# A two-layer transformer kernel: exponentials in pairs, normalisations on ScalarE, a new placing of the small parts, and the first layer's rope rows by repeating transfers

## The reference

```python
# layer 0 attention, 16 heads of 8 dimensions, causal
c_kv = x @ W_kv_down
k_rope = rotary(c_kv @ W_k_rope)          # 32 dimensions, one for all heads
q_rope = rotary(x @ W_q_rope)
scores = q . k + q_rope . k_rope          # per head 8 + 32 dimensions
w = softmax(where(causal, -inf, scores / sqrt(40)))
out = (w @ v) @ W_o
# layer 0 ffn: a shared expert of 512 and 15 routed ones of 256, the best 3 by
# softmax weight, computed densely; plus the residual
# layer 1 attention: 16 heads of 8, no rope, not causal, grouped projections
# layer 1 ffn: 8 experts of 512, layer norm, each token goes to the best one
```

## Time and profile before

| | us |
|---|---|
| median of 3 runs | 984.2 (981.91 to 987.36) |
| profiled execution | 984.84 |
| its span, first to last instruction | 983.1 |
| lead | 0 to 61.1 |
| first layer's attention | 61.1 to 319.2 |
| dense experts | 319.2 to 558 |
| second layer's lead and attention | 558 to 841 |
| drain, blocks, end | 841 to 983.1 |
| PE, DVE, ACT, POOL busy | 792.4, 649.1, 524.2, 344.6 |

### The profile page before, as it was taken

How to read it: one execution, slowest core, us unless ns; L and a number is a source line. 1 busy time by engine, 2 the same in 40 slices (tenths; PEclk the granted TensorE clock), 3 DMA queues, 4 the chain that set the end, 5 groups by cost and what they waited for, 6 DMA issues and landing times. The chain is left out here.

```text
span 983.1 us, 12967 instructions
## 1 busy us (share of the span) xinstructions
PE 792.4 (81%) x4212; PEld 497.0 (51%) x4212; DVE 649.1 (66%) x1290; ACT 524.2 (53%) x970; POOL 344.6 (35%) x389
## 2 busy tenths in 40 slices
PE   3547888988898889999989899789989888527850
PEld 2233444555454667787767544345344444227740
DVE  3135568676663777776768696488898876347853
ACT  1013454545556677776757456456656656217740
POOL 3413775543532000000005345653453542133425
PEclk9987999999999999999999979899999999659985
DMA  4251331102110490000002112210110200011013
GB/s 125 48 95 21 85 81 35 34 22 46 30 24 2 137 285 6 1 1 1 1 8 57 43 42 63 60 35 17 38 25 18 58 4 10 4 54 56 32 34 84
DMA packets 56414, 44.75 MB, mean 46 GB/s; under 512 B 6598, under 2 KB 47387, under 8 KB 56347
## 3 DMA queue, kind: packets, MB, share of 16 engines
q1 hardware_dynamic: 55323, 41.82, 16.8%
q0 software_dynamic: 1024, 2.10, 0.7%
HBM read 14.67 MB, written 14.55 MB: 30 GB/s over the span
## 5 line engine op out<-in xcount | busy, mean ns | idle before, releaser
L926 ACT ACTIVATE ring<-single 128x512 f32<-128x512 f32 (+3 forms) x512 | 253.1, 517 | 226.3 <-PE single L1176 218.8
L1554 DVE TENSOR_REDUCE mneg<-pair 128x2 f32<-128x1024 f32 (+3 forms) x256 | 258.5, 1022 | 87.7 <-PE pair L1160 33.2
L1176 PE MATMUL single<-q_op,k_op 104*128 104x512 f32 (+3 forms) x512 | 216.5, 443 | 17.8 <-ACT ring L926 9.2
L1156 PE MATMUL pair<-k_op,q_op 96*128 96x512 f32 (+3 forms) x512 | 172.1, 415 | 42.2 <-DVE mneg L1554 22.6
L786 POOL TENSOR_SCALAR k_op<-k_stk,cst 104x512 fp32r<-104x512 f32 x64 | 100.0, 1577 | 276.2 <-DMA k_stk<-hl 258.5
L1176 PEld LDWEIGHTS single<-q_op,k_op 122*128 122x128 f32 (+1 forms) x512 | 97.9, 197 | 98.6 <-ACT ring L926 72.6
L1156 PEld LDWEIGHTS pair<-k_op,q_op 120*128 120x128 f32 (+1 forms) x512 | 98.9, 207 | 86.8 <-DVE mneg L1554 44.8
L1192 PE MATMUL p_o<-ring,vaug 128*9 128x512 f32 (+3 forms) x1024 | 116.1, 526 | 1.0 <-ACT ring L926 0.9
L721 POOL TENSOR_SCALAR_AFFINE_SELECT ring<-ring 128x256 f32<-128x256 f32 x128 | 52.3, 408 | 149.4 <-ACT ring L926 149.2
L955 ACT ACTIVATE ring<-pair,cols 128x512 f32<-128x512 f32 x136 | 86.1, 685 | 33.8 <-PE pair L1236 27.5
L1600 DVE TENSOR_TENSOR ring<-ring,single 128x1024 f32<-128x1024 f32 x60 | 73.3, 1221 | 45.5 <-ACT ring L955 44.4
(11 more groups left out here) (294 smaller groups left out, 1306.4 us busy)
## 6 DMA issues: line engine op xcount, KB each, us to landing
xs<-zero SPq DMA_DIRECT2D x10, 1024.0 KB, 10.1
q_op<-hl SPq DMA_DIRECT2D x96, 64.0 KB, 2.0
stage<-in_L_ffn_W_dram SPq DMA_DIRECT2D x8, 512.0 KB, 4.5
stage<-in_L_ffn_rW_dram SPq DMA_DIRECT2D x6, 512.0 KB, 5.1
k_op<-hl SPq DMA_DIRECT2D x48, 64.0 KB
k_stk<-hl SPq DMA_DIRECT2D x48, 64.0 KB, 2.0
xb<-xs SPq DMA_DIRECT2D x15, 128.0 KB, 2.0
xs<-yb SPq DMA_DIRECT2D x15, 128.0 KB, 1.7
```

Of the source, the lines that this page charges most:

```text
L926: exp_done.by(act.activation(ring[:, n % 8, lo:T], singles[n % 2][:, lo:T], ACT.Exp), (L, n))
L1156: ins = pe.matmul(both[:, i, 0:hi], r32(qs[:, P * qt:P * (qt + 1)]), r32(ks[:, 0:hi]), start=i == 0 or L == 1 or qt >= 2, stop=L == 1)
L1176: st_full.by(pe.matmul(singles[n % 2][:, lo:T], r32(ks[:, P * kc:P * (kc + 1)]), r32(qs[:, lo:T]), start=True, stop=True), (L, n))
L1554: s_taken.by(dve.tensor_reduce(mneg[:, G % 2, 2 * p:2 * p + 2, qt], both[:, :, 0:hi], axis=AX.X, op=ALU.max, negate=True), (L, m))
```

## The change

In the first layer:

- `exp_unit` and `exp` work on two heads at a time, in the `pair` buffers, two instructions a quad instead of four; `values` moves to the end of the quad's matmuls.
- `max_unit` uses the `single` buffers. A unit is two heads for the first two blocks of queries and one head for the last two: 12 units a group instead of 8. They stand two to five quads ahead.
- `rope_copy` and `qk_rope` are gone. `head_dma` sends the rope rows itself, by 6 transfers whose source is repeated four times (256 KB each), ahead of the group's 6 head transfers.
- The statistics and Newton steps of rows 1 to 3 are done together at the start of each layer (`BATCH`).

In both layers the application of a normalisation (`P.ne`, `T.ne`, `he`) moves from VectorE (L1392) to ScalarE, as four activations of 128 x 128 with bias and scale; VectorE computes the bias. `TABLE` is new. In the second layer the weight transfers and splits, all in row 0 before, are spread over the rows, at the rows' end on SyncE.

```diff
+SCORES = [[(heads, qt) for p in (0, 2) for heads, qt in (((p, p + 1), 0), ((p, p + 1), 1), ((p,), 2), ((p + 1,), 2), ((p,), 3), ((p + 1,), 3))],
+          [((p, p + 1), qt) for p in (0, 2) for qt in range(NT)]]
...
-        spread = (((-5, (0, 1, 2)), (-4, (3, 4, 5)), (-3, (6, 7))), ((-6, (0, 1)), (-5, (2, 3)), (-4, (4, 5)), (-3, (6, 7))))[L]
+        spread = (((-5, range(0, 4)), (-4, range(4, 7)), (-3, range(7, 10)), (-2, range(10, 12))),
+                  ((-6, (0, 1)), (-5, (2, 3)), (-4, (4, 5)), (-3, (6, 7))))[L]
...
-          (2, "b"): ["mt1", "P.ne"], (2, "d"): ["T.proj"], (3, "b"): ["P.ln1", "T.ns"], (3, "d"): ["P.rp", "T.na"],
...
+TABLE = [{(1, "b"): ["T.ot3"], (2, "b"): ["T.on"], (2, "d"): ["mt1", "U.rt2"], (3, "b"): ["T.proj", "P.ne"], (4, "b"): ["U.gt", "T.ns"],
...
+BATCH = {(0, "b"): "B.s1", (0, "d"): "B.s2", (1, "b"): "B.s3", (1, "d"): "B.sd", (2, "b"): "B.n1", (2, "d"): "B.n2", (3, "b"): "B.n3"}
...
             def head_dma(G):
...
+                if g < 3:
+                    taken.wait_ge(sp, ("rs", r))
+                    for w in range(2):
+                        for t in range(3):
+                            sp.dma_start((q_op0, k_op0)[w][DR * t:DR * (t + 1), GH * s:GH * s + GH, :],
+                                         rope_hl[DR * w:DR * (w + 1), TERM[w][t]:TERM[w][t] + 1, :].broadcast_to([DR, GH, T])).then_inc(rope_rows[s], 16)
...
-                ins = pool.tensor_copy(r32((q_op0, k_op0)[w][0:96, at:at + 2, :]), qk_rope[:, w:w + 1, :].broadcast_to([96, 2, T]))
...
+                    for t in range(NT):
+                        shift, scale = norm_of("P", s, t)
+                        ins = act.activation(xn[:, t, :], x[:, r, t, :], ACT.Identity, bias=shift, scale=scale)
...
-                exp_done.by(act.activation(ring[:, n % 8, lo:T], singles[n % 2][:, lo:T], ACT.Exp), (L, n))
+                    at = 2 * (n % 4)
+                    ins = act.activation(ring[:, at:at + 2, lo:T], pairs[n % 2][:, :, lo:T], ACT.Exp)
...
+                    if L == 0:
+                        exp_unit(L, Q, 0)
+                        for m in waiting[0:2]:
+                            max_unit(L, m)
+                        exp_unit(L, Q, 1)
+                        for name, b in beside_quad(s, q, "b"):
+                            part(name, b)
+                        for m in waiting[2:]:
+                            max_unit(L, m)
+                        if Q:
+                            values(L, Q - 1)
```

More of the change, by code:

```diff
@@ L176, in beside_quad @@
 def beside_quad(a, q, place):
[L177 to L180, removed]
+    L, lo = a // NB, a // NB * NB
+    out = [("wo0", 0)] if (a, q, place) == (0, 1, "d") else []
+    if a == lo and (q, place) in BATCH:
+        out.append((BATCH[q, place], L))
+    return out + [part for entry in TABLE[L].get((q, place), []) for part in named(entry, a, (lo, lo + NB))]
 def beside_unit(v):
     return [part for entry in BESIDE.get(v, [])
-            for part in named(entry, NB if entry[:2] == "T." else NB - 1, (NB - 1, NB + 1))]
+            for part in named(entry, NB if entry[:2] in ("T.", "U.") else NB - 1, (NB - 2, NB + 1))]
 def lead_parts(L):
@@ L403, in build @@
         k_masked = sig("k_masked", list(range(4 * NG)))
-        rope_rows = sem("rope_rows")
+        rope_rows = [sem(f"rope_rows{s}") for s in range(3)]
         m_rows = sem("m_rows")
@@ L421, in unit_scores, with norm_of, rope_fills @@
         def unit_scores(L, m):
-            pair = pairs[m % 2]
-            return pair[:, 0, :].rearrange("p (i k) -> p i k", i=2) if L == 0 and m % 4 < 2 else pair[:, :, :]
+            heads, qt = SCORES[L][m % SU[L]]
+            return pairs[m % 2][:, :, :] if L else singles[m % 2][:, :].rearrange("p (i k) -> p i k", i=len(heads))
+        def norm_of(kind, s, t):
+            i = NT * (s % NB - 1) + t
+            return (nwtB[:, 2, i:i + 1], nwtB[:, 1, i:i + 1]) if kind == "P" and s % NB else (nwt[kind][:, 2, t:t + 1], nwt[kind][:, 1, t:t + 1])
+        def rope_fills(slot, G):
+            return R_ROWS * len([i for i in range(G + 1) if i % 3 == slot and i % NG < 3])
         def x_row(r):
@@ L721, in cut_half @@
                 cut.by(pool.affine_select(tri, tri, [[0, 2], [1, P]], ALU.is_ge, fill, base=0, channel_multiplier=-1), (Q, half))
-            for G in range(3):
-                for w, half in ((0, 0), (0, 1), (1, 0), (1, 1)):
-                    rope_copy(G, w, half)
             for r in range(NB):
@@ L760, in modulate @@
                 else:
-                    rope_set.wait_ge(pool, 14)
+                    for u in range(3):
+                        pool.wait_ge(rope_rows[u], rope_fills(u, 4 * NG - 1))
                 apart(pool)
@@ L875, in part @@
                     if s:
-                        act.wait_ge(rope_rows, R_ROWS * s)
+                        for u in range(3):
+                            act.wait_ge(rope_rows[u], rope_fills(u, NG * s - 1))
                         apart(act)
@@ L1153, in max_unit @@
                 both = unit_scores(L, m)
-                for i in range(2):
-                    qs, ks = operands(L, G, 2 * p + i, 24)
-                    ins = pe.matmul(both[:, i, 0:hi], r32(qs[:, P * qt:P * (qt + 1)]), r32(ks[:, 0:hi]), start=i == 0 or L == 1 or qt >= 2, stop=L == 1)
+                for i, j in enumerate(heads):
+                    qs, ks = operands(L, G, j, 24)
+                    ins = pe.matmul(both[:, i, 0:hi], r32(qs[:, P * qt:P * (qt + 1)]), r32(ks[:, 0:hi]), start=i == 0 or L == 1, stop=L == 1)
                     if L == 0 and qt >= 2:
@@ L1219, in lead @@
                     max_unit(L, m)
[L1220 removed]
+                    if i == SU[L]:
                         part("mt0", NB * L)
@@ L1583, in attention @@
                     waiting = S_AT[L][4 * NG * (s % NB) + q]
-                    for m in waiting[0:1]:
+                    first = (2, 1)[L]
+                    for m in waiting[0:first]:
                         max_unit(L, m)
@@ L1587, in attention @@
                         part(name, b)
-                    for m in waiting[1:]:
+                    for m in waiting[first:]:
                         max_unit(L, m)
```

282 lines of the change are left out of this document (146 added, 136 removed), and 20 rows, old and new, of the table TABLE.

## The result

The change makes the kernel slower: 1034.6 us (median of 4 runs, 1028.0 to 1040.2) against 983.1 (980.6 to 987.4), ratio 1.052, 95% interval 1.044 to 1.059. The forecast was 975, the range 962 to 1000.

The account below looks back on a forecast made before the run. The prediction took the first layer's rows to be bound by handoffs, neither TensorE nor VectorE full. From 984.84 us, +5 (lead) +7 (rope) -17.5 (first layer) -5 (second) +0.5 +0.5 gave -9.5, so 975; range 962 to 1000.

Parts of the forecast that it names:

- Lead: Before the first layer's rows: rope transfers delay the small loads, so VectorE's stop ends later, by 2.3 to 8, taken as +5 us.
- these leave at about 62: In the lead: group 0's maxima leave SyncE at about 62 us instead of 57.2, with group 1 landed at about 59.5.
- +2.3 to +3.1 us by issue alone: In the lead: SyncE's 12 more issues take 7.6 to 8.4 us, of which its free 5.3 us take up most.
- Rope rows: First layer, steady state: nine groups' rope rows land late for TensorE's fourth quad, net 0.8 us each, +7 us.
- Need 13.7 and room 11.9: First layer: a group's rope and head transfers need 13.7 us, TensorE leaves room for 11.9, so 1.8 us late.
- would be spent waiting for maxima anyway: First layer's groups: some 1 us of the 1.8 us lateness coincides with TensorE's wait for maxima, leaving net 0.8.
- worth nothing by itself: First layer: removing GpSimd's 36 rope copies gains nothing, since GpSimd waits for ScalarE most of the time.
- Rival 1: Rope transfers are slow: at 1.6 us each a group is 3.7 us late net, total about 1004 us; chance 27%.
- Pairs, singles, places and batch in the first layer: First layer's rows: fewer waits for ScalarE, VectorE and inside chains, less later maxima; sum -17.5 us, bounds -26 and -5.
- Second layer: Second layer's attention: shorter mask wait, normalisations off VectorE and parts spread; -5 us, bounds -9 and +3.
- ScalarE's 1.1 us pieces may take it back: Second layer: normalisations on ScalarE, 1.1 us each, may cancel the gain of about 0.6 us in each of three rows.
- If these are 3 us or more the first rival holds: Sign in first layer's rows: fourth-quad waits for head or rope rows, expected under 2 us, would at 3 show slow transfers.

Follow-up runs that it names:

- e7: Changed kernel, but after the first three groups each rope transfer writes one head's rows only, 64 KB instead of 256: 1005.7 us.
- e10: Changed kernel with the third group's rope and head transfers in the lead behind the first maxima and small loads: 1032.1 us.
- e9: Changed kernel with the second layer as before and rope rows by plain transfers, behind the third group's maxima, and later GpSimd copies: 972.4 us.
- e14: e9 with the first layer's normalisations on VectorE too, so none is left on ScalarE: 980.1 us.
- e12: Changed kernel with the second layer's normalisations on VectorE and its weights back in row 0; its new table and batched statistics stay: 1023.8 us.
- e13: e9 with the second layer's weight pieces spread over the rows, GpSimd's modulation and scatter kept ahead of the masks: 972.6 us.
- e5: Changed kernel with the second layer's normalisations alone moved back to VectorE: 1021.8 us.
- e1: Changed kernel with rope rows as before, by plain transfers ahead of the third group's maxima and GpSimd copies: 1018.4 us.
- e4: Changed kernel with rope rows by copies, sent ahead of the third group's maxima, and the second layer as before: 995.2 us.

## Why the prediction was wrong

- **Lead, +5 against +15.3.** The group's time was right (12.2 us worked out, 11.6 measured), and so was the link from the small loads to VectorE's stop. The failed step is "these leave at about 62": it has the maxima leave once group 1 has landed. On SyncE's queue the third group's 12 transfers stand ahead of them, and the sum "+2.3 to +3.1 us by issue alone" took issues at the pace of plain ones. Here an issue waited for transfers ahead of it, as e7's short issues show: three groups at 11.6 are 35 us where rope and head rows together took 17. e10 shows what stood behind them, with the first exponential 12 us sooner.
- **Rope rows, +7 against +23 to +28.** The transfer was sized well. Need 13.7 and room 11.9 were forecast, 14.2 and 11.4 measured in the group shown; that makes 1.8 us late into 2.8, 9 us over nine groups. The failed step is the offset, that 1 us "would be spent waiting for maxima anyway": e9 waits 2.2 us for the maxima's transfer in the whole layer, and with short transfers (e7) TensorE's other waits were 9.2 us against 8.4 in the changed kernel, so hardly any was hidden. The sum has no term for what a stop costs beyond itself, the 7 to 13 us by which TensorE's matmuls take longer in the kernels with the stops, at the lower clock. And one term was put at nothing: the end of GpSimd's copies was to be "worth nothing by itself", but e9 with the copies has 10 us more of other waits than e7 without them. It fits that the rows lost 23 us against the kernel with copies and 28 against e7. Rival 1 came nearest, but for the wrong reason: it wanted 1.6 us a transfer. With head issues at their 0.70 us the lead's 11.6 us leave 7.4 for six rope transfers, 1.2 each as an estimate. The prediction's 1.85 us took the number of engines from the Trainium skill's rule ("DMA: Bandwidth & Descriptors", section "Why a DMA increments its semaphore by 16 and not by 1") and the pace of each from the head rows. The trace does not bear that pace out; a DMA share of 0.84 over rope and head rows, for 0.55 with head rows alone, agrees with more engines at work.
- **Pairs, singles, places and batch in the first layer, -17.5 against -15.1** in the rows of e9. The sum held, with ScalarE's normalisations part of it (8 us by e14). Its parts were not tested one by one, and two of them were off in opposite directions: the wait for the maxima's transfer, priced at 3.5 us a row, is 2.2 us in the whole layer, and the waits for VectorE's reductions, of which half were to go, are 7.2 us. So the close agreement is partly luck. The dense stage was put at +0.5; it came out between +0.5 and +6 in the kernels with the new first layer, and why is open.
- **Second layer, -5 against +22.4.** The wait for masks fell as said, and e12 and e13 show that this is worth 3 to 5 us at most. The failed step is "ScalarE's 1.1 us pieces may take it back": the piece is 1.64 us (four of 482 ns each that overlap), ahead of an exponential, with TensorE one or two exponentials from a stop since the layer has single buffers and single heads. That is 13 us by e5; that the single buffers make the difference is argued, not shown. The places and the batch, credited with 0.6 us a row, cost another 15 together. The sign that the prediction had named, a second layer changed by more than 9 us, showed.
- Of the terms only the second layer's had the wrong sign; the others that missed were too small. The test "If these are 3 us or more the first rival holds" was a poor one: the nine waits had a mean of 2.8 us, and the transfers cost 36.

## What to carry to other kernels

A longer transfer can cost its time twice: once where its rows are wanted, and once for everything queued behind it. Here the issues behind four-fold transfers took 3.54 us for 2.20. Read the queue's order to its end before a price is put on an issue. A part moved to an engine with idle time is not free if that engine's own consumers stand close behind it: the same normalisation on ScalarE gained 8 us in the first layer, which works in pairs, and lost 13 in the second with its single buffers. The layers differ in more than that, so take the buffers as the first thing to look at and not as a rule. And when a part is taken back for an experiment, look for waits that its old place makes in the new order: here such a wait hid 20 us.

## What the runs showed that was not expected

- The exchange of copies for transfers cost 55 us in the old structure and 36 in the new one; with the wait that e1 and e4 carry it seemed to cost 13 to 16.
- Eighteen small instructions of VectorE on `nwtT`, in the first layer's rows, took 8.3 us in e9 with GpSimd's copies and 3.3 in e7 without them.
- An activation with scale and bias as operands took 482 ns where an exponential of the same 128 columns took 276.
- Seven executions with the same first layer spread by 8 us in it when TensorE stopped nine times for transfers; e9 and e13, with hardly such stops, had 240.9 and 242.8.
